# A graph network's last stage on one Trainium2 core: order of the final scatter products, one product in two parts, and one addition for three vector outputs

## The reference

```
x  = x + A_norm @ (relu(layernorm(x)) @ W0) + bias          # first layer
h  = relu(layernorm(x))                                     # second layer from here
s, v   = projections of h to 32 scalars and 32 3-vectors, gathered at the edges' sources
Wf     = filter network of the edge attributes              # per edge, 32 x 6
edge   = products of s, v, the edge's direction and Wf      # 2 scalars and 2 vectors of 32 are used
agg    = segment_sum(edge, node)                            # 256 nodes
os1    = ssp(s_in @ w_f2o1_s / sqrt(64)),  ssp(z) = softplus(z) - ln 2
os2    = os1 @ w_f2o2_s / sqrt(128)
ov2    = (v_in @ w_f2o1_v) @ w_f2o2_v, for each of 3 components, scaled
x  = x + concat(os2 (128 columns), ov2 (128 x 3 columns, the component fastest))
```

## Time and profile before

| | |
|---|---|
| median of 3 runs | 71.74 us (71.64 to 71.81) |
| the profiled execution, its own time | 71.83 us |
| its span, first to last instruction | 69.8 us |
| PE busy / PEld busy | 61.7 us (88%) / 48.6 us (70%) |
| DVE busy | 60.1 us (86%) |
| ACT busy / POOL busy | 48.6 us (70%) / 39.5 us (57%) |
| mean granted TensorE clock | 0.988 of full speed |

### The profile page before, as it was taken

The page is one execution under the profiler, slowest core; times in us unless marked ns, Lnnn a source line. Parts: engine busy times, 40 slices in busy tenths (PEclk is TensorE's granted clock), DMA queues, the critical chain, the costliest instruction groups (busy, mean ns, idle before and its releaser), DMA issues.

```text
span 69.8 us, 1215 instructions
## 1 busy us (share of the span) xinstructions
PE 61.7 (88%) x407; PEld 48.6 (70%) x407; DVE 60.1 (86%) x124; ACT 48.6 (70%) x74; POOL 39.5 (57%) x46
## 2 busy tenths in 40 slices
PE   3999998999999999897998979999999999998340
PEld 1236754568834268796987969998898989997220
DVE  4599999999979968989999898989898999972760
ACT  0700059978999697967979999988696969732700
POOL 5000030000676989594799979999999988700000
PEclk9999999999999999999999999999999999999995
DMA  0899998984000000000000000000000000000044
GB/s 1 129 396 247 361 499 379 449 317 124 9 0 0 0 0 0 0 0 5 0 0 0 0 0 9 5 0 0 0 0 0 0 0 9 0 0 0 0 148 153
DMA packets 3049, 5.65 MB, mean 81 GB/s; under 512 B 540, under 2 KB 1936, under 8 KB 2916
## 3 DMA queue, kind: packets, MB, share of 16 engines
q1 hardware_dynamic: 2274, 5.14, 21.3%
q10 hardware_dynamic: 770, 0.44, 2.2%
HBM read 5.06 MB, written 0.52 MB: 80 GB/s over the span
## 4 chain that ended last, share of the span: by engine, by line
DVE 45%; PE 20%; issue 14%; ACT 13%; DMA 3%; DVEq 0%; ACTq 0%
ACT OsR L240 8%; DVE WQ L412 7%; DVE Os L412 7%; PE pair L632 5%; ACT w_sb L284 5%; DVE dst_bc L565 4%; PE pair L733 4%; PE pair L742 4%; DVE pair L514 3%; PE pair L674 3%; DMA idx_sb<-idx 3%; PE pair L721 3%; DVE w_sb L485 2%; DVE za L446 2%; DVE hX L449 2%
## 5 line engine op out<-in xcount | busy, mean ns | idle before, releaser
L733 PE MATMUL pair<-OsR,Mh 128*128 128x256 f32 x56 | 13.6, 281 | 0.0
L733 PE MATMUL pair<-OsR,Ml 128*128 128x256 f32 x56 | 13.6, 281 | 0.0
L721 PE MATMUL pair<-HL,OdT 128*128 128x256 f32 x68 | 10.1, 289 | 1.6 <-DVE dst_bc L565 0.7
L395 POOL TENSOR_TENSOR Ml<-dst_bc,Mh 128x512 fp32r<-128x512 f32 x8 | 10.4, 1305 | 1.1 <-ACT Mh L301 1.0
L721 PEld LDWEIGHTS pair<-HL,OdT 128*128 128x128 f32 x68 | 8.6, 188 | 2.8 <-issue 2.8
L733 PEld LDWEIGHTS pair<-OsR,Ml 128*128 128x128 f32 x56 | 10.5, 188 | 0.0
L733 PEld LDWEIGHTS pair<-OsR,Mh 128*128 128x128 f32 x56 | 10.5, 188 | 0.0
L605 PEld LDWEIGHTS pair<-WQ,Os 128*128 128x128 bf16 x68 | 6.8, 104 | 4.0 <-DVE WQ L412 1.8
L605 PE MATMUL pair<-WQ,Os 128*128 128x256 bf16 x68 | 9.4, 297 | 0.2 <-DVE WQ L412 0.2
L399 POOL TENSOR_TENSOR Ml<-dst_bc,Mh 128x512 fp32r<-128x512 f32 x7 | 9.2, 1309 | 0.0
L240 ACT ACTIVATE OsR<-Os 128x1024 fp32r<-128x1024 bf16 (+1 forms) x9 | 9.0, 999 | 0.0
(11 more groups left out here) (122 smaller groups left out, 140.2 us busy)
## 6 DMA issues: line engine op xcount, KB each, us to landing
dst_bc<-dst_row SPq DMA_DIRECT2D x1, 2176.0 KB, 12.9
w_sb<-w SPq DMA_DIRECT2D x1, 1024.0 KB, 8.1
x_sb<-x SPq DMA_DIRECT2D x1, 512.0 KB, 4.4
out<-x_sb SPq DMA_DIRECT2D x2, 192.0 KB, 1.9
f_sb<-f_t SPq DMA_DIRECT2D x1, 378.0 KB
b_sb<-bias SPq DMA_DIRECT2D x1, 256.0 KB, 13.1
w_sb<-w ACTq DMA_DIRECT2D x1, 128.0 KB, 4.1
out<-x_sb ACTq DMA_DIRECT2D x1, 128.0 KB, 1.9
```

The source lines that it names most:

```text
L395: nc.gpsimd.tensor_tensor(Ml[:, o, 0:n, feats(1)], M[:, o, 0:n, feats(1)], Mh[:, o, 0:n, feats(1)].bitcast(fp32), ALU.subtract).then_inc(q ...
L721: last = nc.tensor.matmul(gpair[g % 2][:, j * 2 * C:(j + 1) * 2 * C], OdT[:, a, t * P:(t + 1) * P], HL[:, a, :, :], start=(a == 0), stop=( ...
L733: last = nc.tensor.matmul(bank[4 + b][:, 0:N], part[:, g % RG, j, feats(b)], OsR[:, g % RG, j, :], start=(TG * g + j == 0 and part is Mh), ...
```

## The change

Four things are changed, all from the last scatter products on.

1. The order of the scatter products of groups 7 and 8: Mh of A7, Mh of B7, Mh of B8, Ml of A7, Mh of A8, Ml of A8 (`scatA`), Ml of B7, then the wait for `aggA` and the product `os1`, and only then Ml of B8 (`scat`).
2. Aggregate 1 is copied by DVE, not ACT. The copy stands in DVE's stream between the copy of aggregate 0 and the operation for `te2`.
3. The vector products: component 0 for both halves first, then component 2 for both, then component 1 for both. Each component-1 product waits for the component-2 product of its half (a new semaphore `fin2`). All three now lie side by side in `bank[a]`, and one DVE addition of 384 columns for each half takes the place of two.
4. The second product of the scalar branch: `te2` times `o2s` for both halves, then `ta` (ACT's Ln) times `o2s`, added in PSUM. The DVE addition into `os1T` is gone. `te2` is scaled as before.

```diff
-            act.wait_ge(q["scat"], NG)
-            nc.scalar.activation(aggT[:, 1, :], bank[5][:, 0:N], ACT.Copy).then_inc(q["aggT"], 1)
             act.wait_ge(q["os1"], 1)
...
             nc.vector.tensor_copy(aggT[:, 0, :], bank[4][:, 0:N]).then_inc(q["aggA"], 1)
+            dve.wait_ge(q["scat"], NG)
+            nc.vector.tensor_copy(aggT[:, 1, :], bank[5][:, 0:N]).then_inc(q["aggT"], 1)
             dve.wait_ge(q["ta"], 1)
             nc.vector.tensor_scalar(te2[:], bank[2][:, 0:N], SF, 0.0, ALU.mult, ALU.max).then_inc(q["rl"], 1)
             for a in range(NH):
                 dve.wait_ge(q["fin"], a + 1)
-                ov = o_sb[:, a, B:].rearrange("p (d c) -> p c d", c=3)
-                xv = x1[:, a, B:].rearrange("p (d c) -> p c d", c=3)
-                xz = bank[a][:, 0:2 * B].rearrange("p (c d) -> p c d", c=2)
-                nc.vector.tensor_tensor(ov[:, 0:3:2, :], xz, xv[:, 0:3:2, :], ALU.add)
-                nc.vector.tensor_tensor(ov[:, 1, :], bank[6 + a][:, 0:B], xv[:, 1, :], ALU.add).then_inc(q["ov"], 1)
-                if a == 0:
-                    dve.wait_ge(q["tl"], 1)
-                    dve.wait_ge(q["rl"], 1)
-                    nc.vector.tensor_tensor(os1T[:], te2[:], ta[:], ALU.add).then_inc(q["os1T"], 1)
+                nc.vector.tensor_tensor(o_sb[:, a, B:].rearrange("p (d c) -> p c d", c=3),
+                                        bank[a][:, 0:3 * B].rearrange("p (c d) -> p c d", c=3),
+                                        x1[:, a, B:].rearrange("p (d c) -> p c d", c=3), ALU.add).then_inc(q["ov"], 1)
...
             pe.wait_ge(q["OsR"], LATE)
+            pe.wait_ge(q["MhA"], LATE)
+            scatter_part(LATE - 1, 0, Mh)
             pe.wait_ge(q["MhB"], LATE)
             scatter_part(LATE - 1, 1, Mh)
-            pe.wait_ge(q["MhA"], LATE)
-            scatter_part(LATE - 1, 0, Mh)
-            pe.wait_ge(q["MlB"], LATE)
-            scatter_part(LATE - 1, 1, Ml)
             pe.wait_ge(q["OsR"], LATE + 1)
             pe.wait_ge(q["MhB"], LATE + 1)
             scatter_part(LATE, 1, Mh)
+            pe.wait_ge(q["MlA_late"], 1)
+            scatter_part(LATE - 1, 0, Ml)
             pe.wait_ge(q["MhA"], LATE + 1)
             scatter_part(LATE, 0, Mh)
-            pe.wait_ge(q["MlA_late"], 1)
-            scatter_part(LATE - 1, 0, Ml)
             pe.wait_ge(q["MlA_late"], 2)
             scatter_part(LATE, 0, Ml).then_inc(q["scatA"], 1)
-            pe.wait_ge(q["MlB_late"], 1)
-            scatter_part(LATE, 1, Ml).then_inc(q["scat"], 2)
+            pe.wait_ge(q["MlB"], LATE)
+            scatter_part(LATE - 1, 1, Ml)
 
             pe.wait_ge(q["aggA"], 1)
             pe.wait_ge(q["o1"], 1)
             nc.tensor.matmul(bank[2][:, 0:N], o1s_sb[:], aggT[0:64, 0, :], start=True, stop=True).then_inc(q["os1"], 1)
+            pe.wait_ge(q["MlB_late"], 1)
+            scatter_part(LATE, 1, Ml).then_inc(q["scat"], 2)
+            pe.wait_ge(q["wcs"], 1)
+            for a in range(NH):
+                nc.tensor.matmul(bank[a][:, 0:B], aggT[64:128, 0, a * P:(a + 1) * P], wc_sb[64:128, :], start=True, stop=True)
             pe.wait_ge(q["aggT"], 1)
-            pe.wait_ge(q["wcs"], 1)
+            for a in range(NH):
+                nc.tensor.matmul(bank[a][:, 2 * B:3 * B], aggT[64:128, 1, a * P:(a + 1) * P], wc_sb[64:128, :], start=True,
+                                 stop=True).then_inc(q["fin2"], 1)
+            for a in range(NH):
+                pe.wait_ge(q["fin2"], a + 1)
+                nc.tensor.matmul(bank[a][:, B:2 * B], aggT[0:64, 1, a * P:(a + 1) * P], wc_sb[0:64, :], start=True,
+                                 stop=True).then_inc(q["fin"], 1)
             pe.wait_ge(d_o2s, 16)
-            for a in range(NH):
-                n = slice(a * P, (a + 1) * P)
-                nc.tensor.matmul(bank[a][:, 0:B], aggT[64:128, 0, n], wc_sb[64:128, :], start=True, stop=True)
-                nc.tensor.matmul(bank[a][:, B:2 * B], aggT[64:128, 1, n], wc_sb[64:128, :], start=True, stop=True)
-                nc.tensor.matmul(bank[6 + a][:, 0:B], aggT[0:64, 1, n], wc_sb[0:64, :], start=True,
-                                 stop=True).then_inc(q["fin"], 1)
-            pe.wait_ge(q["os1T"], 1)
-            for a in range(NH):
-                n = slice(a * P, (a + 1) * P)
-                nc.tensor.matmul(bank[2 + a][:, 0:B], os1T[:, n], o2s_sb[:], start=True, stop=True).then_inc(q["os2"], 1)
+            pe.wait_ge(q["rl"], 1)
+            for a in range(NH):
+                nc.tensor.matmul(bank[2 + a][:, 0:B], te2[:, a * P:(a + 1) * P], o2s_sb[:], start=True, stop=False)
+            pe.wait_ge(q["tl"], 1)
+            for a in range(NH):
+                nc.tensor.matmul(bank[2 + a][:, 0:B], ta[:, a * P:(a + 1) * P], o2s_sb[:], start=False,
+                                 stop=True).then_inc(q["os2"], 1)
```

More of the change, by code:

```diff
@@ L132, in gnn_preln_kernel @@
         wc_sb = sb("wc_sb", [P, B])
-        ta, te, te2, os1T = (za[:, i * N:(i + 1) * N] for i in range(4))
+        ta, te, te2 = (za[:, i * N:(i + 1) * N] for i in range(3))
         o_sb = x_sb
@@ L149, in gnn_preln_kernel @@
                  "G Glo add vys Q svw red MA MhA MhB MlA MlB MlA_late MlB_late scat "
-                 "scatA aggA aggT wc wcs o1 os1 ta te tl rl os1T fin os2 ov o")
+                 "scatA aggA aggT wc wcs o1 os1 ta te tl rl fin2 fin os2 ov o")
         q = {n: sem("s_" + n) for n in names.split()}
```

## The result

The kernel after takes 72.20 us (median) against 71.73 for the kernel before; the ratio is 1.0059, 95% interval 1.0033 to 1.0086. That is 0.42 us slower (0.24 to 0.62), clear of the 0.2% that such a measurement can tell. Forecast were +0.39 us.

The account below looks back on a forecast made before the run. It took one chain without slack as the bound: scatter products, copy of aggregate 0, `os1`, ACT, then DVE's 2.51 us. DVE's additions start 0.91 later and its work saves 0.52: net 0.39 slower, 72.13 us, range 71.72 to 72.45.

Parts of the forecast that it names:

- The stall at Ml of A7: Reordered scatter products: PE waits for DVE's Ml of A7 until 61.75, losing 0.24 of the 0.47 us gained.
- the lateness at Mh of A7: First reordered scatter load: input ready for 60.36 against 60.33, 0.03 us late, swallowed by the next stall.
- The gap behind `os1`: PE going from 64-row `os1` to 128-row Ml of B8: an open load of 0.12 us, bounds 0 to 0.29.
- Rival B: Full array drain at each change between 64 and 128 rows: 0.29 us behind `os1`, 72.30 us; chance 0.20.
- The late copy and the wait between the vector products: Aggregate 1 copied 1.14 us later, component 1 waiting for component 2: DVE's first addition at 66.14, 0.91 later.
- The addition: DVE's 384-column vector addition: 0.66 us long, 0.57 from start to start, 0.08 saved twice, 0.18 with rounding.
- `os1T` gone, products under the additions: Scalar branch: DVE saves 0.34 us; PE's longer second product is hidden by the additions, in time by 0.15.
- The sum: DVE's tail: 0.52 us saved, started 0.91 later, net 0.39 slower, DVE ending at 67.79.
- the time outside the span: Time not in the profiled span: last stores keep their distance from landing, nothing counted for it.
- Rival C: PE's product ends seen earlier (0.10 each) and no gap behind `os1`: 0.24 us faster, 71.50 us; chance 0.10.
- Rival D: Same time: additions at the unstrided rate (0.11 less, twice), no gap behind `os1` (0.12 less), 71.79 us; chance 0.12.

Follow-up runs that it names:

- the last kernel: Kernel after with Ml of B8 back ahead of `os1`, no 64-row products (padded and diagonal weights), component 0 before the aggregate 1 wait, zeros late: 70.82 us, ratio 0.9870.

## Why the prediction was right

Right in sign, size and mechanism. Step by step:

- *The stall at Ml of A7*: forecast load at 61.75, it is at 61.74. The pause ahead of it is about 0.15, not 0.24, because the first load comes at 60.41 and not at 60.33: the lateness at Mh of A7, put at 0.03, is 0.08. As foreseen, the stall swallows it. The copy of aggregate 0 forecast at 63.01, it is at 63.00; `os1` forecast at 63.49, it is at 63.48. The run of the order alone confirms that this is a gain by itself.
- *The gap behind `os1`*: this term was mis-sized. I took 0.12 between bounds of 0 and 0.29. The load of Ml of B8 starts at 64.11 and its products end at 64.61 where 64.55 was forecast: the gap is 0.18 to 0.20. It has two parts: the load waits until about 0.10 after the array has taken the last column of `os1` (64.11 against 63.80 + 0.21, the second record's start by the spacing of before), and then it lies in the open. The run of `os1` on 128 rows shows that both vanish when the rows don't change. Rival B was right that the change of rows costs, and too dear by 0.1: its full price would have had the copy at 64.76, it was at 64.65. It had PE wait for the whole tail of `os1`, but the load starts 0.07 ahead of the modelled end (64.18). The Trainium skill ("TensorEngine Tiling (Array Packing)", § Tiling Modes) says that a change of the tiling mode drains TensorE. The runs agree with it in kind: the change cost 0.20 us on the chain, and without it the wait was gone.
- *The late copy and the wait between the vector products*: forecast first addition 66.14, it is 66.19; the idle time of DVE ahead 0.81, it is 0.79.
- *The addition*: forecast 0.57 from start to start, it is 0.59 (67.37 - 66.19 = 1.18 for two). One takes 0.68 where 0.66 was read from the rows of 256 and 128 columns; the unstrided 0.549 would have been 0.13 off.
- *`os1T` gone, products under the additions*: forecast to be in time by 0.15, and DVE did not wait. The two-part product alone gave 0.43 where 0.34 of addition were counted, within its interval; its tail is 0.38 shorter.
- *The sum*: DVE's end forecast at 67.79, it is 67.37 + 0.49 = 67.86: the first addition starts 0.05 later (the gap) and the two additions take 0.04 more, the last two operations 0.02 less. That makes 0.46 where 0.39 were forecast for DVE's end, 0.42 in the ratio, 72.20 us where 72.13 were forecast. The forecast took the time outside the span as unchanged, without a reason. It is about 2.0 us in both kernels, but up to 0.3 away from that in four of the kernels above; that it cancelled here was luck.

Rival C (ends seen earlier than modelled) fell: DVE's copy starts 0.04 after the modelled end of Ml of B8 (64.61, 64.65). Rival D needed a free gap and the unstrided rate; neither came.

## What to carry to other kernels

Moving work behind an urgent instruction is free only as far as the slack of the branch that waits for that work reaches: here component 1 of half 0 was complete 1.50 us later (66.16 against 64.66), 0.57 us of slack stood against that, and about 0.95 came through. The fix was to move two matmuls back. A change of several parts is worth measuring in parts: order and two-part product gain (0.2 and 0.43 us), the wide addition gains nothing alone, and one misplaced pair of products hid it all. Padding a half-height product with zero rows, or laying its weights on a diagonal, can shorten such a tail, because the waits at a change between 64 and 128 rows and between the vector products go: the padding alone took 0.20 us off the tail of the kernel after, both together 0.14 off that with Ml of B8 moved alone. With component 0 in the wrong place the second tail was 0.13 longer instead, and for the padding alone the whole time did not fall measurably.

## What the runs showed of the hardware

A 128-row product directly behind a 64-row one got its weight load only about 0.10 us after the array had taken the last column, and its result 0.20 us later than behind a product of 128 rows. The reverse change waits too: component 0 in the kernel after loads at 64.54, where Ml of B8's second product started at 64.61 - 0.28 = 64.33 and took 0.12 to stream. Two kernels above show it with and without the change. With Ml of B8 moved alone, `os1` on 64 rows loads at 63.57, 0.18 after its input is copied (62.97 + 0.42 = 63.39), behind a last scatter product that started at 63.36. In the last kernel `os1` has 128 rows and loads at 63.29, 0.06 after the copy (62.81 + 0.42 = 63.23), with a last scatter product from 63.20.

Products on the upper and on the lower 64 rows run beside each other: eight records of 128 columns took 0.72 us where the four of one component alone took 0.71. A wait between them, or weights that need all 128 rows, gives that up.

DVE's three remainders took 1.35 us in every kernel but the two with diagonal weights, where POOL's writes and copies of these weights ran at the same time: 1.45 and 1.54. That one caused the other is not shown, and the tail did not wait for it.

The time outside the span isn't constant from kernel to kernel: about 2.0 us for the kernels before and after (1.97 to 2.10), 2.25 to 2.30 and 2.21 to 2.29 in the two with the zeros written at the start, 2.08 to 2.18 with them late, 1.74 to 1.87 in the two kernels with diagonal weights, of which one writes its zeros at the start too. So early zeros alone don't lengthen it. Within one kernel it keeps to about 0.1. What makes it is open: the added instructions, their place, the added semaphores and the shifted addresses were not tried apart. It is as large as the effects looked for, so an effect on one chain should be read in the span and the timeline before the whole time is believed. It also flatters the fastest kernel by about 0.2 of its 0.9 us; its median span of 69.0 against 69.6 is the rest.
